# One core, four gated layers: how the values of attention 2 are made, and where a bias split and one exponential stand

## The reference

```python
x = x + tanh(g_xattn[L]) * xattn_L(layernorm(x), ctx)
x = x + tanh(g_ffn[L])   * ffn_L(layernorm(x))
```

```python
k, v = jnp.split(ctx @ w_kv, 2, axis=-1)      # w_kv is 128 x 16, so v is 8 wide
out  = softmax(band(q @ k.T)) @ v
```

## Time and profile before

| | |
|---|---|
| median of 3 runs | 687.5 us (686.61 to 687.59) |
| profiled execution, its own time | 688.58 us |
| its span, first to last instruction | 686.8 us |
| busy share: TensorE / VectorE / ScalarE / GpSimd | 91% / 74% / 54% / 33% |
| mean granted clock of TensorE | 0.97 of full speed |

### The profile page before, as it was taken

One profiled execution on the slowest core, in us unless ns is written; L12 is line 12 of the kernel. 1 busy time (PEld: TensorE's weight loads), 2 busy tenths in 40 slices (PEclk: granted clock), 3 DMA queues, 4 the chain that ended last, 5 costly groups with the idle time before them and its releaser, 6 DMA issues.

```text
span 686.8 us, 11700 instructions
## 1 busy us (share of the span) xinstructions
PE 626.2 (91%) x3547; PEld 440.9 (64%) x3571; DVE 505.7 (74%) x1287; ACT 368.3 (54%) x635; POOL 229.1 (33%) x438
## 2 busy tenths in 40 slices
PE   8888999978999799988997899999987999969996
PEld 6665777646766467755665467777665777645774
DVE  7675988979774479878545598888769888456886
ACT  6244454434766345525672377777733665623774
POOL 3210566341002125621121047666530000202673
PEclk9997999999999989999999899999999999997999
DMA  8243111010000001110003011111010000000111
GB/s 280 85 134 129 36 47 35 24 46 3 26 4 3 24 0 43 40 32 2 4 5 70 0 33 38 46 38 38 24 32 3 3 26 3 2 1 1 47 38 39
DMA packets 21358, 25.47 MB, mean 37 GB/s; under 512 B 3842, under 2 KB 18850, under 8 KB 21308
## 3 DMA queue, kind: packets, MB, share of 16 engines
q1 hardware_dynamic: 20732, 23.83, 11.8%
q10 hardware_dynamic: 576, 1.02, 0.4%
HBM read 20.58 MB, written 3.77 MB: 35 GB/s over the span
## 4 chain that ended last, share of the span: by engine, by line
PE 73%; DVE 16%; ACT 4%; issue 3%; DMA 1%; POOL 1%; DVEq 0%; SPq 0%; ACTq 0%
PE PS L653 12%; PE PS L655 11%; PE PS L654 11%; PE PS L675 5%; PE PS L885 4%; PE PS L794 4%; PE PS L868 3%; PE PS L504 3%; DVE negmax L1555 2%; DVE consts L1561 2%; PE PS L900 2%; DVE qst L1515 2%; PE PS L865 1%; DVE pT L1460 1%; PE PS L841 1%
## 5 line engine op out<-in xcount | busy, mean ns | idle before, releaser
L407 POOL TENSOR_TENSOR wpair<-ring,ones_col 128x128 fp32r<-128x128 f32 (+1 forms) x150 | 79.3, 529 | 170.7 <-PE PS L655 124.3
L1460 DVE TENSOR_TENSOR pT<-pT,PS 128x512 f32<-128x512 f32 x150 | 102.5, 684 | 28.9 <-ACT pT L1064 23.0
L1163 ACT ACTIVATE pT<-PS 128x512 f32<-128x512 f32 x160 | 92.0, 592 | 50.7 <-PE PS L868 41.5
L1466 DVE TENSOR_TENSOR hid_lo<-pT,hid_hi 128x512 fp32r<-128x512 f32 x150 | 109.3, 729 | 2.5 <-ACT hid_hi L1071 1.6
L409 POOL TENSOR_TENSOR wpair<-ring,wpair 128x128 fp32r<-128x128 f32 (+1 forms) x150 | 100.4, 669 | 11.8
L1071 ACT ACTIVATE hid_hi<-pT 128x512 fp32r<-128x512 f32 x150 | 93.7, 624 | 12.4 <-DVE pT L1460 11.7
L653 PE MATMUL PS<-hid_hi,wpair 128*128 128x512 f32 x150 | 85.8, 572 | 4.4 <-DVE hid_lo L1466 4.4
L653 PE MATMUL PS<-xhi,wpair 128*128 128x512 f32 x204 | 85.5, 419 | 1.9 <-DVE pT L1460 1.7
L1064 ACT ACTIVATE pT<-PS,ring 128x512 f32<-128x512 f32 x96 | 65.9, 688 | 36.8 <-PE PS L655 36.8
L655 PE MATMUL PS<-xhi,wpair 128*128 128x512 f32 x204 | 83.2, 408 | 0.0
L654 PE MATMUL PS<-xlo,wpair 128*128 128x512 f32 x204 | 82.9, 406 | 0.0
(11 more groups left out here) (233 smaller groups left out, 1135.8 us busy)
## 6 DMA issues: line engine op xcount, KB each, us to landing
ring<-in_mlp SPq DMA_DIRECT2D x48, 128.5 KB, 2.1
ring<-in_glu SPq DMA_DIRECT2D x27, 192.0 KB, 2.4
kz<-keys SPq DMA_DIRECT2D x36, 96.0 KB
keys<-qst SPq DMA_DIRECT2D x6, 512.0 KB, 3.9
qst<-kfull SPq DMA_DIRECT2D x96, 4.0 KB
wq<-in_wq SPq DMA_DIRECT2D x3, 256.0 KB, 3.5
x_res<-in_x SPq DMA_DIRECT2D x1, 512.0 KB, 4.7
ctx_tok<-in_ctx_tok SPq DMA_DIRECT2D x1, 512.0 KB, 6.2
```

Of the source, the lines that this page charges most:

```text
L407: pool.tensor_tensor(wpair[:, pair, 0, c], w, ones, ALU.mult).then_inc(M["wstep"], 1)
L1163: act.activation(pT[:, w % 8, :], PS[:, 2 + w % 2, :], ACT.Exp, scale=sc).then_inc(A["p"], 1)
L1460: dve.tensor_tensor(hid[:, hf, :], src[:, hf, :], PS[:, 6 + hf, :], ALU.mult).then_inc(M["hid"], 1)
L1466: dve.tensor_tensor(hid_lo[:, kept, :], hid[:, kept % 2, :], hid_hi[:, kept, :].bitcast(f32), ALU.subtract).then_inc(M["lo"], 1)
```

## The change

- **Values of attention 2.** TensorE makes them by token tiles: eight matmuls, one for each 128 tokens of `ctxT`, four behind each half of the layer norm's transposes (`window_tiles`). A tile is the window that starts at 0 or at 128, so ScalarE copies the eight tiles to windows 0 and 3 of each batch, behind the layer norm's copies. The windows that start at 32 and at 96 lie across two tiles: SyncE puts them together by four DMAs from windows 0 and 3 within on-chip memory (`shift_windows`), behind the saving of the last keys and ahead of the masks. Attention 2 waits for these (`v_in`) before its first product with values. In the list `chunks` the values of attention 2 move from place 10 to place 6, and the keys of 3 and 2 go one place back.
- **Bias splits.** The eight instructions of VectorE that split `b2` move from `prepare_routing` to behind the five frequency products.
- **Exponential.** On ScalarE the exponential of the lags moves ahead of the two `key_high` copies of attention 1.

```diff
@@ chunks
-                  + [("k", 3, 0), ("k", 3, 1), ("k", 2, 0), ("k", 2, 1), ("v", 2, 0)])
-        KV_MIX, KV_LN = 2, 6
+                  + [("v", 2, 0), ("k", 3, 0), ("k", 3, 1), ("k", 2, 0), ("k", 2, 1)])
+        KV_MIX, KV_LN, KV_V2 = 2, 7, 6
-        keys_done = {1: 2, 3: 8, 2: 10}
+        keys_done = {1: 2, 3: 9, 2: 11}
@@ SyncE
+            def shift_windows():
+                win = vall[2][:, :, 0, :].rearrange("p (b n) c -> p b n c", n=NW)
+                sp.wait_ge(kv_out, KV_V2 + 1)
+                sp.wait_ge(vall_set, 6)
+                for n in (1, 2):
+                    first = P - WSTART[n]
+                    sp.dma_start(win[0:first, :, n, :], win[P - first:P, :, 0, :]).then_inc(v_in, 16)
+                    sp.dma_start(win[first:P, :, n, :], win[0:P - first, :, NW - 1, :]).then_inc(v_in, 16)
@@ SyncE, load_ring(0)
                     for K in (3, 2):
                         save_keys(K)
+                    shift_windows()
                     sp.wait_ge(ac["kfreq"], 2)
                     sp.dma_start(mask_i[:, 0, :, :], t["mask_q"]).then_inc(ld_mask, 16)
@@ TensorE
-                elif L == 2:
-                    for i in range(B * NW):
-                        mm = pe.matmul(o[:, i * HD:(i + 1) * HD], ctxT[:, in_window(i // NW, i % NW)], wv[2][:, :], start=True, stop=True)
+            def window_tiles(hf):
+                if hf == 0:
+                    pe.wait_ge(ld_att[2], 32)
+                    pe.wait_ge(kv_out, KV_V2 - 1)
+                for i in range(4 * hf, 4 * hf + 4):
+                    mm = pe.matmul(PS[:, 6 + KV_V2 % 2, i * HD:(i + 1) * HD], ctxT[:, i * P:(i + 1) * P], wv[2][:, :],
+                                   start=True, stop=True)
+                if hf == 1:
+                    mm.then_inc(kv_mm, 1)
@@ TensorE, autocorrelation
-                for n in range(KV_MIX, KV_LN):
+                for n in range(KV_MIX, KV_V2):
                     key_value(n)
@@ TensorE, experts(0)
-                    key_value(len(chunks) - 1)
@@ TensorE, attention 2, first product with values
                         pe.wait_ge(A["qe"], pre["qe"] + adds["qe"])
+                        pe.wait_ge(v_in, 64)
@@ TensorE, main
             layer_norm(1, (0,))
+            window_tiles(0)
             route(0, 0)
             layer_norm(1, (1,))
+            window_tiles(1)
             route(0, 1)
@@ ScalarE, values
-                    act.activation(vall[2][:, :, 0, 0:HD], PS[:, 6 + n % 2, 0:B * NW * HD].rearrange("p (t d) -> p t d", d=HD),
+                    act.activation(vall[2][:, :, 0, 0:HD].rearrange("p (b n) d -> p b n d", n=NW)[:, :, 0:NW:NW - 1, :],
+                                   PS[:, 6 + n % 2, 0:NT * HD].rearrange("p (b t d) -> p b t d", b=B, d=HD),
@@ ScalarE, main
+            act.wait_ge(ac["top"], 1)
+            act.activation(cw[:, 1, :], cw[:, 0, :], ACT.Exp).then_inc(ac["exp"], 1)
             for n in range(0, KV_MIX):
                 key_high(n)
-            act.wait_ge(ac["top"], 1)
-            act.activation(cw[:, 1, :], cw[:, 0, :], ACT.Exp).then_inc(ac["exp"], 1)
...
-            for n in range(KV_MIX, KV_LN):
+            for n in range(KV_MIX, KV_V2):
                 values(n)
             layer_norm(1)
+            values(KV_V2)
             spread_picks()
             route(0)
...
-            values(len(chunks) - 1)
             experts(0, True)
@@ VectorE, prepare_routing
+            def prepare_biases():
                 for L in (2, 3):
                     link(dve.tensor_copy(b2part[L][:, 0, :], b2[L][:, :]))
                     link(dve.tensor_tensor(b2rest[:, :], b2[L][:, :], b2part[L][:, 0, :], ALU.subtract))
                     link(dve.tensor_copy(b2part[L][:, 1, :], b2rest[:, :]))
                     link(dve.tensor_tensor(b2part[L][:, 2, :], b2rest[:, :], b2part[L][:, 1, :], ALU.subtract))
@@ VectorE, autocorrelation, behind L1334
                 dve.tensor_tensor(prod[:, 4, :], prod[:, 2, :], prod[:, 3, :], ALU.subtract).then_inc(ac["prod"], 1)
+                prepare_biases()
```

More of the change, by code:

```diff
@@ L211, in build @@
         k_saved = [None] + [sem(f"k_saved{L}") for L in range(1, 4)]
+        v_in = sem("v_in")
         kz_set, kz_flag, kz_in = sem("kz_set"), sem("kz_flag"), [sem(f"kz_in{b}") for b in range(B)]
```

## The result

The changed kernel took 683.21 us (median of 6 executions, 681.47 to 684.22); the kernel before, on the same chip, 687.55 (6 executions, 686.61 to 689.27). The ratio is 0.9932, with a 95% interval of 0.9913 to 0.995. The gain is 4.3 us where 8.9 were forecast, and 683.2 lies above the range of 676.3 to 681.9. The profiled execution had 681.47 us, with a span of 679.7.

A forecast was written before the change was run, and what follows sets the result against it. TensorE was taken to carry 73% of the chain, with three serial pieces holding up what follows. Head 1.24, values 4.88 and clock 2.81 made 8.93 us, off 687.5 giving 678.6 us; range 676.3 to 681.9.

The forecast's parts named there:

- Then the splits until 23.02: VectorE before the search for lags: bias splits, priced at 2.32 us, follow products and difference; correlation starts 1.24 us earlier.
- the head gives nothing: Rival: splits hold VectorE as long as before and the key rests eat the exponential's gain; 679.8 us, chance 0.08.
- the head: Stretch up to the mix's copy, with bias splits and exponential moved: everything behind it comes 1.24 us earlier.
- Exponential first: ScalarE ahead of the key copies: mix arrives 1.42 us earlier, but ScalarE is last, so the head gains 1.24.
- Tiles in the gaps: TensorE before the routing products: the tile matmuls fit into idle gaps of 1.55 and 1.41 us, cost 0.
- The values leave the start of stage 0: TensorE before L642: the values of attention 2 and a 0.18 us wait go, 4.88 us besides the head's 1.24.
- What the clock gives back: Start of stage 0: full clock instead of half once the 8-column stretch is gone, 2.81 us more.
- The clock rival: Clock falls anyway, or in a later lull: 1.5 us per half-clock stretch, 680.1 or 681.6 us, chance 0.27.
- DMAs: Four SyncE issues of 1,024 small packets ahead of masks and ring loads: cost 0, at most 2 us.

The follow-up runs named there:

- values_only: The changed kernel with bias splits and exponential back in their old places; ratio 0.9923 to the kernel before.
- splits_idle: The changed kernel with the bias splits moved on to behind the mix, where VectorE waits; ratio 0.9900 to the kernel before, 0.9912 when repeated.
- exp_back: splits_idle with the exponential back behind the two key copies; 680.35 us, ratio 0.9900 to the kernel before.
- exp_only: The kernel before with only the exponential moved ahead of the two key copies; ratio 0.9996.
- wide_columns: The kernel before with 128 columns instead of 8 in the 32 instructions that make the values of attention 2; ratio 0.9974.
- head_only: The kernel before with only the bias splits moved behind the products and the exponential ahead of the key copies; ratio 1.0013.
- changed_third: The changed kernel run a third time, beside other runs on their chip; 682.47 us, ratio 0.9936 to the kernel before.
- pool_late: The changed kernel with GpSimd's first weight splits held until the lags' difference is done; ratio 0.9914 to the kernel before.

## Why the prediction was wrong, step by step

**"Then the splits until 23.02": failed, in its size.** The start of the step was right: the correlation began at 18.36 (18.29 forecast) with no idle, the difference was done at about 20.7. But the splits were priced at 2.32 us, their durations in a place where GpSimd stood still, and moved to where GpSimd splits weights. They took 3.6 to 4.5 us in the traces of kernels that have them there, so the correlation's 1.24 us turned into a loss at the search: 25.13 against 23.69. VectorE's idle 0.78 us at L1351 is gone and gives back about half of these 1.44: 0.68 are left at the mix and at the first routing product. The rival "the head gives nothing" named the effect (splits that hold VectorE) but bounded it at 0; it goes below. GpSimd's rows from 20 us on were in the trace of before. They should have been read when work was moved beside them. The step's price: 1.24 us forecast, -0.63 measured (changed against values_only, means, standard error 0.45; -0.4 with each against the kernel before on its own chips). That it gained the 1.24 is excluded; that it lost anything at the end is likely and not certain. With the splits in idle time the head gives 1.08 (splits_idle) to 1.47 (exp_back) over values_only, as forecast.

The Trainium skill, "SBUF — State Buffer", section "Who interferes with whom", says that of the engines only VectorE and GpSimd get in each other's way, over a pair of memory ports that they share and that one of them holds for an instruction's whole length. The traces agree in kind: the bias splits stretch from 2.31 to 4.48 us, and the search, whose values come from PSUM, keeps its 0.43 us beside GpSimd in exp_back. A size for such a mix of short instructions only the runs gave. The prediction did not weigh this rule.

**Exponential first: right in kind, empty in value.** The prediction saw that ScalarE, not the mix, is late at L1208. It followed that the exponential brings nothing of its own there, and exp_only measured 0.0. The 1.24 for the head therefore hung on the splits alone.

**Tiles in the gaps: held.** 0.76 and 0.62 us of idle time are left ahead of the routing halves, where 1.55 and 1.41 had been.

**The values leave the start of stage 0: held, but a part of it is the clock's.** From the keys of attention 3 to the transposes are 11.15 us before and 6.20 after, 4.95 less for 4.88 forecast. At full clock the removed work is 3.67 + 0.18 = 3.85 us; the other 1.03 of the 4.88 were half clock.

**What the clock gives back: mechanism right, size off.** The fall behind the 8-column products is gone, and from the first loop product to the third spread are 3.11 us (60.74 to 63.85), as in the earlier trace rows. In this pair of traces the term even came out: from the keys of attention 3 to the third spread are 19.69 us before and 11.94 after, 7.75 less for the 4.88 + 2.81 = 7.69 forecast. But the 2.81 us, with the 1.03 above, 3.84 in all, are the price of one execution, in which the fall lasted 10.2 us. Over many, half clock drops from 40.3 to 34.0 us. In the 62 executions of before, time rises by 0.27 us with each us of half clock (correlation 0.81), so this is an estimate of 1.7 us in place of 3.84; wide_columns, which takes the same fall away and leaves the products, measured 2.0 (1.0 to 3.1). Values and clock: 3.85 + 1.7 = 5.55; measured 5.61; forecast 7.69. The clock rival had the rest, "falls in a later lull where it did not": in the profiled execution the new stretch at 133 us took back 1.5 us (15 idle products in 4.81 us, where before they took 3.40), and the first fall was longer. That stretch is no single accident: of the 14 traces of kernels with the values moved, 9 have a fall beginning at 130 to 135 us, of the 4 with the values in their old place only head_only has one at the end of stage 0. No run tests why.

The Trainium skill, "TensorE: Matmul & The Clock Gate", section "What's actually happening", has the monitor running freely, so that falls need not stand at the same work in each execution. The runs agree: splits_idle and splits_idle_2 are the same kernel, and the second fall came at 158.5 us in one trace and at 130.8 in the other; of the three traces of the changed kernel only changed_third fell at 31.8. The fall at the second routing half is steadier, from 42.1 to 45.9 us in 16 of 18 traces. A price taken from one trace's fall is a draw from that spread.

**DMAs: held.** The four issues took 0.60 to 0.70 us each on SyncE and landed in 1.8 to 2.5. The first ring load was issued at 67.45, later than the 64.3 forecast, and no product waited for it: TensorE has no idle from 61 to 130 us. Attention 2 needs the windows after 300 us, when they had long landed.

**The sum.** Forecast 1.24 + 4.88 + 2.81 = 8.93. Means: -0.63 + 3.85 + 1.7 = 4.9, measured 4.98 (standard error 0.3). The -0.63 is itself a difference of measured means, so what the sum tests is the values' part, 5.55 against 5.61. Of the 4.0 us missing, 1.9 are the head's, and 2.1 are the clock's, priced by a single execution. Two small slips of the prediction change nothing here: its range reaches 0.3 us beyond its cases at each end (681.9 where two half-clock stretches give 681.6), and the chances it counts as faster add up to 0.97, not 0.96.

Open: why splits_idle with fillers doesn't lose the fall at 43; whether fillers sized for one lull at a time would bring anything; and how much of the difference between executions of one kernel (682.47 and 680.84 as medians of the same program) is the arrival of the first expert weights, which sets GpSimd's start (19.1 to 20.1 us), and how much the clock.

## What to carry to other kernels

When work moves to another time, read not only what its own engine does there but, for VectorE and GpSimd, what the other does: an instruction's duration belongs to its neighbours too. A clock fall seen in one trace is worth its mean over executions, not its length in that one, and the rows within it are already priced at half clock, so take the removed work at full clock and the clock as a term of its own. For small work with no near deadline, such as these table splits, look for a wait of the engine to put it in, rather than for another place on the path.

## What the runs showed of the hardware

- VectorE and GpSimd slowed each other on short instructions: on VectorE casts of 96x128 took up to 0.63 us instead of 0.22 and subtractions 0.83 instead of 0.29 (changed kernel against pool_late); on GpSimd a 128x256 product took up to 1.08 instead of 0.61.
- Not all VectorE work is hit: the search (MAX8 from PSUM) took 0.43 us with GpSimd at work (exp_back) and without (pool_late).
- 32 instructions of 8 columns and 32 of 128 columns took nearly the same time at full clock, 0.11 us each. Behind the former the granted clock was 0.50 in all three traces that have them ahead of stage 0, behind the latter 1.00 (wide_columns).
- 1,024 packets of 36 bytes within on-chip memory went in four transfers; each landed 1.8 to 2.5 us after its issue, and nothing that could be seen waited for them.
- In the executions of the kernel before, a us more of half clock went with 0.27 us more of time. Idle products in the lulls brought half clock down to 26.8 us from the 35.0 of splits_idle, but the kernel became 3.2 us slower.
